# Causal attention on one core: the projections move into the attention slots, two head groups ahead, and each score tile gets a PSUM bank of its own

## The chip, the cores and the metric

The program runs on one core of a Trainium2 chip. The metric is the device time of one execution in microseconds; lower is better. Engines are named as in the profile: PE is TensorE, PEld its weight loads, DVE is VectorE, ACT is ScalarE, POOL is GpSimd, SP is the engine whose queue issues most DMAs.

## What is computed

Eight sequences of 1024 tokens, width 512, 16 heads of 32. An attention block, a layer norm, a mixture of 16 experts that each pick their tokens, a second layer norm. Only the attention block is touched:

```python
q = split_heads(x @ Wq.T + bq)
k = split_heads(x @ Wk.T + bk)
v = split_heads(x @ Wv.T + bv)
q_lr = jnp.einsum('bhtd,hdr->bhtr', q, Wq_lsr)
k_lr = jnp.einsum('bhtd,hdr->bhtr', k, Wk_lsr)
scores = jnp.einsum('bhir,bhjr->bhij', q_lr, k_lr) * scale
scores = jnp.where(causal_mask, jnp.float32(-jnp.inf), scores)
attn = jax.nn.softmax(scores, axis=-1)
y = jnp.einsum('bhij,bhjd->bhid', attn, v)
x = _layernorm(x + y @ Wo.T + bo)
```

## The kernel before

`build_attention` handles one sequence after the other (a "batch" in the code). The 16 heads go in four groups (`GROUPS`) of four heads (`HG`). One group is one **slot** of the program, and a batch is four slots and a **tail**.

For a group the kernel needs: the **projections** of its queries and keys ("proj", four of 12 matmuls each, every operand split into a high and a low float32r part); copies of them, the **strips**, which 24 DMAs on SP's queue bring from the tile `natural` into `q_operands` and `k_operands`, six per head, two buffers by the group's parity; the **row maxima** of the scores ("max", 48 matmuls whose tiles DVE reduces), joined and transposed ("maxT") and sent by two small DMAs into a row of `q_operands`, which is what `m_sent` counts; and the **core**: for 12 steps k the transposed scores of four heads ("scores"), their exponential on ACT, and two products, with the values ("values") and with ones for the denominators ("sums"). The denominators are inverted on DVE in four pieces and multiplied in on POOL.

The tail has for each of eight token tiles t the output product ("out"), layer norm 1 on DVE, the value projection of the next batch ("v"), the transposes of the normalised rows ("turn") and router logits ("logit").

PE's order is a list that `plan_batch` builds. All engines walk the same list, each taking its own part. In a slot g before the change come the four projections of group g+1, then the core of g, in which the 48 maxima of g+1 are spread evenly from step k=3 on, then maxT. Projections, maxima, maxT and the whole tail use two PSUM banks in turn (`shared`); a bank is free again when ACT or DVE has read it. The scores use four banks in two pairs: a pair holds two heads, and one ACT instruction of 1024 columns takes both. On the diagonal (8 of the 12 steps, so 32 score tiles in a slot) a matmul with `mask_k` adds the causal mask (line 630).

SP's queue holds DMAs in the order of its own code: strips, the weights of the next projection (`load_w`, 1 MB into the one buffer `wqk_group`), the next batch's x (`load_x`, into `natural`), and in the tail the residual rows (`x_residual`, two buffers) and the stores. POOL adds the bias to a residual tile before DVE may use it. SP, like every engine, does not go past an instruction that waits.

Of the kernel before, what the change touches and what calls it, by code (L numbers as in the profile page):

```python
# [15 lines left out]
P = 128  # L16
# [154 lines left out]
def plan_batch():  # L171

    order = []
    for g in range(GROUPS):
        order += plan_step(g, True)
    order += plan_tail()

    e = len(attend_steps())  # L180
    for g in range(GROUPS):
        n = order.index(("values", g, e - 1))
        order[n:n + 3] = [order[n + 2], order[n], order[n + 1]]
    return order


TURN_LAG = 2


def plan_tail():  # L190

    order = []
    for t in range(TT + TURN_LAG):
        if t < TT:
            order += [("out", t), ("v", t)]
        if t >= TURN_LAG:
            order.append(("turn", t - TURN_LAG))
            if (t - TURN_LAG) % QT == QT - 1:
                order.append(("logit", (t - TURN_LAG) // QT))
    return order  # L200


# [18 lines left out]
LEAD = 3  # L221
TAIL = 4


def attend_parts(g, k, e):


    parts = [("scores", g, k, 0), ("scores", g, k, 1)]
    for n in ([k - 1] if k > 0 else []) + ([k] if k == e - 1 else []):
        parts += [("values", g, n), ("sums", g, n)]  # L230
    return parts


def plan_step(g, attend):


    order = [("proj", g, i) for i in range(4)]
    e, m = len(attend_steps()) if attend else 0, len(max_steps())
    if not attend:
        return order + [("max", g, i) for i in range(m)] + [("maxT", g)]  # L240
    parts = [part for k in range(e) for part in attend_parts(g, k, e)]
    first, final = parts.index(("scores", g, LEAD, 0)), len(parts) - TAIL
    done = 0
    for n, part in enumerate(parts):
        order.append(part)
        if first <= n < final:
            share = m * (n + 1 - first) // (final - first)
            order += [("max", g, i) for i in range(done, share)]
            done = share
        if n == len(parts) - 3:  # L250
            order.append(("maxT", g))
    assert done == m
    return order


def build_attention(nc, w, x_dram, xT_dram, x1_dram, table, logits_dram, scratch, keep, NB):
    with ExitStack() as ctx:
# [80 lines left out]
        def turns(order, base):  # L338

            at, n = {}, base  # L340
            for item in order:
                if uses_bank(item):
                    at[item] = (n % 2, n // 2)
                    n += 1
# [1303 lines left out]
```

## Time and profile before

| | |
|---|---|
| median of 3 runs | 4426.57 us (4421.46 to 4427.38) |
| profiled execution | 4426.47 us, span 4424.7 us |
| PE busy | 3971.2 us, 90% of the span |
| PEld busy | 2624.6 us, 59% |
| DVE busy | 2281.6 us, 52% |
| ACT busy | 1423.9 us, 32% |
| POOL busy | 482.2 us, 11% |

The span is the time from the first to the last instruction of the profiled execution. Busy shares are averages over the whole program. The attention block takes roughly the first 2610 us of it; experts and the last layer norm fill the rest. Matmuls are pipelined, so "busy" counts overlapping pieces once and the distance from one matmul's start to the next says more than the length of either.

### The profile page before, as it was taken

Reading aid. Unit: us, or ns where it says so; the run is one execution under the profiler, and the core shown is the slowest. Engines: PE = TensorE matmul, PEld = TensorE weight load, DVE = VectorE, ACT = ScalarE, POOL = GpSimd, SP = SyncE. Lnnn points to the kernel's source line nnn. Section 1 sums busy time; section 2 is a strip of 40 time slices with the busy share of each in tenths; the row PEclk is TensorE's granted clock in tenths of the full one; section 3 lists DMA queues with packets and bytes.
Section 4 is the critical chain, followed back from the end, with each engine's and each line's share of the span. In section 5 each row is a group of like instructions: output and inputs, shape, how many; then the busy total and the mean of one; then the engine's idle time right before and its main releaser. Section 6 shows DMA issues by size and latency. Waiting matters only on the chain. (4 is left out here: it accounts for less than half of the span.)

```text
span 4424.7 us, 62103 instructions
## 1 busy us (share of the span) xinstructions
PE 3971.2 (90%) x22505; PEld 2624.6 (59%) x22505; DVE 2281.6 (52%) x3990; ACT 1423.9 (32%) x1986; POOL 482.2 (11%) x349
## 2 busy tenths in 40 slices
PE   5999999999999999999999971689999999999990
PEld 4545555555555455545555531578888888888880
DVE  2565455554554554554564546645444544454444
ACT  1233333332332332333333330133333333333324
POOL 2011011011011010011010010001111111111100
PEclk7899999999999999999999995589999999999995
DMA  4232323332331332133222310044433443344328
GB/s 139 61 84 87 76 70 96 79 79 76 77 101 56 76 101 82 51 100 92 66 82 84 73 55 8 7 138 129 126 117 117 126 129 117 117 125 130 117 67 313
DMA packets 187361, 423.09 MB, mean 96 GB/s; under 512 B 39776, under 2 KB 42848, under 8 KB 178400
## 3 DMA queue, kind: packets, MB, share of 16 engines
q1 hardware_dynamic: 167408, 367.98, 27.5%
q0 software_dynamic: 14336, 34.09, 4.1%
q10 hardware_dynamic: 5376, 17.83, 1.0%
q8 instruction: 149, 2.44, 0.2%
q14 instruction: 92, 0.75, 0.1%
HBM read 245.70 MB, written 72.38 MB: 72 GB/s over the span
## 5 line engine op out<-in xcount | busy, mean ns | idle before, releaser
L798 DVE TENSOR_REDUCE max_slots<-shared_banks 128x1 f32<-128x512 f32 (+3 forms) x1536 | 805.7, 550 | 632.6 <-PE shared_banks L581 535.6
L742 ACT ACTIVATE probs<-scores_t 128x1024 f32<-128x1024 f32 (+3 forms) x768 | 613.0, 811 | 907.4 <-PE scores_t L630 531.5
L1471 PE MATMUL m_ps_h<-m_tokens_t,m_w_parts 128*128 128x512 f32 x3072 | 739.8, 391 | 1.6 <-DVE m_tokens_t L1409 1.6
L1471 PE MATMUL m_ps_y<-m_w_parts,m_hidden_parts 128*128 128x512 f32 x3072 | 737.1, 390 | 0.5
L578 PE MATMUL shared_banks<-k_operands,q_operands 96*128 96x512 f32 (+3 forms) x1536 | 618.7, 431 | 63.9 <-DVE max_slots L798 52.7
L1471 PEld LDWEIGHTS m_ps_y<-m_w_parts,m_hidden_parts 128*128 128x128 f32 x3072 | 575.5, 188 | 125.3 <-issue 6.3
L1471 PEld LDWEIGHTS m_ps_h<-m_tokens_t,m_w_parts 128*128 128x128 f32 x3072 | 575.4, 188 | 120.1 <-issue 2.0
L578 PEld LDWEIGHTS shared_banks<-k_operands,q_operands 96*128 96x128 f32 x1536 | 295.9, 196 | 522.8 <-DVE max_slots L798 346.0
L627 PE MATMUL scores_t<-q_operands,k_operands 128*128 128x512 f32 (+3 forms) x1536 | 507.9, 403 | 21.3 <-ACT probs L742 15.4
L1378 ACT ACTIVATE m_hidden<-m_ps_h,m_b 128x512 f32<-128x512 f32 x256 | 176.7, 690 | 817.7 <-PE m_ps_h L1471 804.6
L1436 DVE CAST m_hidden_parts<-m_hidden 128x512 fp32r<-128x512 f32 x256 | 111.3, 435 | 584.1 <-ACT m_hidden L1378 584.1
L611 PE MATMUL shared_banks<-x_parts,wqk_group 128*128 128x512 f32 x1536 | 382.1, 406 | 22.1 <-issue 20.4
L611 PEld LDWEIGHTS shared_banks<-x_parts,wqk_group 128*128 128x128 f32 x1536 | 294.5, 195 | 95.6 <-issue 28.3
L627 PEld LDWEIGHTS scores_t<-q_operands,k_operands 128*128 128x128 f32 x1536 | 290.0, 198 | 88.6 <-issue 47.9
L647 PE MATMUL y_bank<-probs,v_rows 128*32 128x512 f32 (+3 forms) x3072 | 336.1, 510 | 0.0
L647 PE MATMUL den_bank<-probs,ones_f 128*32 128x512 f32 (+3 forms) x3072 | 328.9, 500 | 0.0
L493 POOL TENSOR_TENSOR y_cols<-y_cols,denominators 128x512 f32<-128x512 f32 x64 | 82.0, 1281 | 1660.5 <-DVE denominators L826 1660.5
L611 PE MATMUL shared_banks<-wo_cols,y_cols 128*128 128x512 f32 x512 | 236.9, 606 | 15.7 <-DVE ln_stats L837 8.1
L581 PE MATMUL shared_banks<-mask_q_rows,ident_bf 128*128 128x128 bf16 x1024 | 242.3, 237 | 0.0
L1336 POOL DMA_INDIRECT scratch_x<-m_out,m_idx x64 | 114.0, 1781 | 1142.9 <-DVE m_out L1455 1128.3
L826 DVE RECIPROCAL denominators<-denominators 128x128 f32<-128x128 f32 x256 | 235.9, 936 | 2.2
L630 PE MATMUL scores_t<-mask_k_rows,ident_bf 128*128 128x128 bf16 x1024 | 230.6, 231 | 0.0
(206 smaller groups left out, 3318.2 us busy)
## 6 DMA issues: line engine op xcount, KB each, us to landing
m_w_raw<-in_w1T SPq DMA_DIRECT2D x64, 1024.0 KB, 5.1
m_w_raw<-in_w2T SPq DMA_DIRECT2D x64, 1024.0 KB, 7.3
q_operands<-natural SPq DMA_DIRECT2D x384, 128.0 KB, 2.4
k_operands<-natural SPq DMA_DIRECT2D x384, 128.0 KB, 2.5
wqk_group<-scratch_wqk SPq DMA_DIRECT2D x32, 1024.0 KB, 5.2
natural<-in_xT SPq DMA_DIRECT2D x8, 2048.0 KB, 7.6
x_residual<-in_x SPq DMA_DIRECT2D x64, 256.0 KB, 2.7
scratch_x<-probs SPq DMA_DIRECT2D x64, 256.0 KB, 2.0
```

The lines of the kernel that those rows point to most:

```text
L578: mm = pe.matmul(out[:, 0:n], q_ops[0:MAX_STRIP, buf, h, it * P:(it + 1) * P], k_ops[0:MAX_STRIP, buf, h, k0:k0 + n], start=True, stop=not ...
L581: mm = pe.matmul(out[:, n - P:n], identb[:], mask_q[:], start=False, stop=True)
L611: mm = pe.matmul(out, a, c, start=(n == 0), stop=(n == len(pairs) - 1))
L627: mm = pe.matmul(out[:, c0:HALF], k_ops[:, buf, h, j * P:(j + 1) * P], q_ops[:, buf, h, hh * HALF + c0:(hh + 1) * HALF], start=True, stop= ...
L630: mm = pe.matmul(out[:, c0:c0 + P], identb[:], mask_k[:], start=False, stop=True)
L647: mm = pe.matmul(bank[h * DH:(h + 1) * DH, c0:HALF], rows(h, j), probs[:, slot_of(k, h // 2), h % 2, c0:HALF], start=(j == 0), stop=(j == ...
L742: act.activation(probs[:, slot_of(k, pair), :, c0:HALF], st[:, pair, :, c0:HALF], ACT.Exp, scale=SCALE).then_inc(exp_done, 1)
L798: dve.tensor_reduce(mx[:, h, slot:slot + 1], src[:, 0:n], AX.X, ALU.max).then_inc(bank_free[bank], 1)
L826: dve.reciprocal(den[:, cols], den[:, cols]).then_inc(rden_ready, 1)
L1336: pool.indirect_dma_start(out=x1_dram[:, :], out_offset=bass.IndirectOffsetOnAxis(ap=idx[:, r, j:j + 1], axis=0), in_=out[:, j, :], in_off ...
L1378: act.activation(h[:, f % 2, :], ps_h[:, f % 2, 0:CAP], ACT.Gelu, bias=b1[:, r, f:f + 1]).then_inc(gelu_done, 1)
L1471: mm = pe.matmul(bank, a, b, start=(first and n == 0), stop=(final and n == len(pairs) - 1))
```

## The change

The projections of a group are made two slots ahead and inside the core, two of them after part 46 and two after part 57 of the 60 parts of a slot. The strips then go into the buffer that the running core still reads, so SP waits for the slot's last score tile (`st_full`) before it issues them. The 48 maxima are placed by a table, the first of them after part 5, that is after the second head of step k=1. Scores have four single banks: one matmul, one ACT instruction and one wait for each head. The causal mask is no longer a matmul; POOL zeroes the upper triangle of the probabilities after the exponential (`mask_probs`, one instruction for two heads), and "values" of a diagonal step waits for it. "values" and "sums" of a step stand side by side. The pieces of the inversion have fixed places. The next batch's x is split on POOL in eight pieces during slot 2. On SP's queue one set of strips, for group 1 of the next batch, now stands in the tail. The lead-in makes two groups and mixes values, projections and maxima.

```diff
-LEAD = 3
-TAIL = 4
-        if n == len(parts) - 3:
-            order.append(("maxT", g))
+AHEAD = 2
+MAX_AFTER = (0, 0, 0, 0, 0, 2, 1, 1, 0, 1, 1, 0, 0, 1, 0, 1, 0, 0, 5, 2,
+             3, 1, 2, 0, 1, 1, 0, 1, 1, 1, 1, 0, 2, 2, 0, 0, 0, 1, 3, 2,
+             2, 0, 2, 1, 0, 1, 1, 0, 1, 1, 0, 1, 1, 0, 0, 0, 0, 0, 0, 0)
+PROJ_AFTER = (46, 46, 57, 57)
+JOIN_AFTER = 55
...
+    for k in range(e):
+        parts += [("scores", k, h) for h in range(HG)]
+        if k > 0:
+            parts.append(("weigh", k - 1))
...
+            order += [("values", g, part[1]), ("sums", g, part[1])]
...
-        st = ps("scores_t", [P, 2, 2, HALF])
+        st = ps("scores_t", [P, SCORE_BANKS, HALF])
...
-            def strips(b, g, lead=False):
-                await_parts(sp, sp_passed, b, (g - 1) % GROUPS, lead)
+            def strips(b, slot, lead=False):
+                await_parts(sp, sp_passed, b, slot, lead)
+                g = (slot + AHEAD) % GROUPS
+                if not lead:
+                    plain(sp, st_full, (b * GROUPS + slot + 1) * NE * HG, sp_passed)
...
                 if more:
-                    load_x(b + 1, n0 + GROUPS)
-                    load_w(0)
-                    strips(b, 0)
+                    load_x(b + 1, b * GROUPS + GROUPS)
+                    strips(b, GROUPS - 2)
                     load_w(1)
-                for t in range(TT + TURN_LAG):
+                load_residual(b, 0)
+                if more:
+                    strips(b, GROUPS - 1)
+                    load_w(2)
+                for t in range(1, TT + TURN_LAG):
...
+            def mask_probs(b, g, k, pair):
+                c0 = steps[k][2]
+                s = (b * GROUPS + g) * NE + k
+                block = probs[:, slot_of(k, pair), :, c0:c0 + P]
+                plain(pool, exp_done, HG * s + 2 * pair + 2 + SCORE_BANKS, pool_passed)
+                pool.affine_select(out=block, in_=block, compare_op=ALU.is_ge, fill=0.0, base=0,
+                                   pattern=[[0, 2], [1, P]], channel_multiplier=-1).then_inc(masked, 1)
...
-                for q in range(2):
-                    h = 2 * pair + q
-                    out = st[:, pair, q, :]
-                    diag = j * P >= hh * HALF
-                    mm = pe.matmul(out[:, c0:HALF], k_ops[:, buf, h, j * P:(j + 1) * P],
-                                   q_ops[:, buf, h, hh * HALF + c0:(hh + 1) * HALF], start=True, stop=not diag)
-                    if diag:
-                        mm = pe.matmul(out[:, c0:c0 + P], identb[:], mask_k[:], start=False, stop=True)
-                mm.then_inc(st_full, 1)
+                pe.wait_ge(exp_done, s + 1)
+                pe.matmul(st[:, (HG * k + h) % SCORE_BANKS, c0:HALF], k_ops[:, buf, h, j * P:(j + 1) * P],
+                          q_ops[:, buf, h, hh * HALF + c0:(hh + 1) * HALF], start=True, stop=True).then_inc(st_full, 1)
...
+                if diagonal[k]:
+                    pe.wait_ge(masked, (b * GROUPS + g) * N_DIAG + masked_through(k))
```

What this does to the order is seen at three places. The first is PE's order from the end of one slot into the next, before the change; the line numbers are those of the kernel before (L611 projections, L647 values and sums, L627 scores, L630 their mask).

```order
L647 MATMUL y_bank<-probs,v_rows 32x128 x4
L647 MATMUL den_bank<-probs,ones_f 32x128 x4
L611 MATMUL shared_banks<-x_parts,wqk_group 128x512 x12
L527 REGISTER_ALU
L611 MATMUL shared_banks<-x_parts,wqk_group 128x512 x24
L620 REGISTER_ALU
L622 ISA
L627 MATMUL scores_t<-q_operands,k_operands 128x512
L630 MATMUL scores_t<-mask_k_rows,ident_bf 128x128
```

The same place after the change (L670 projections, L701 values and sums, L682 scores):

```order
L670 MATMUL shared_banks<-x_parts,wqk_group 128x512 x12
L693 REGISTER_ALU
L701 MATMUL y_bank<-probs,v_rows 32x256 x4
L701 MATMUL den_bank<-probs,ones_f 32x256 x4
L693 REGISTER_ALU
L694 ISA
L701 MATMUL y_bank<-probs,v_rows 32x128 x4
L701 MATMUL den_bank<-probs,ones_f 32x128 x4
L679 REGISTER_ALU
L681 ISA
L682 MATMUL scores_t<-q_operands,k_operands 128x512
```

The last projection of a slot, whose result the strips carry, stood right ahead of the next slot's scores; now the products of steps 10 and 11 stand between.

The second place is the start of a slot on PE after the change, from the fourth head of step 0 on. L637 is a maximum, L640 its mask.

```order
L682 MATMUL scores_t<-q_operands,k_operands 128x512
L681 ISA
L682 MATMUL scores_t<-q_operands,k_operands 128x384
L681 REGISTER_ALU
L682 MATMUL scores_t<-q_operands,k_operands 128x384
L634 REGISTER_ALU
L637 MATMUL shared_banks<-k_operands,q_operands 128x128
L640 MATMUL shared_banks<-mask_q_rows,ident_bf 128x128
L584 REGISTER_ALU
L637 MATMUL shared_banks<-k_operands,q_operands 128x256
```

The first maximum, which waits for head 0 of the strips, now comes after six score tiles; before, the scores of steps 0 to 2 and half of step 3 and the products of steps 0 to 2 stood ahead of it.

The third place is SP's queue around the start of the tail. Before, the last strips and the weights were followed by the two first residual loads:

```order
L387 DMA wqk_group<-scratch_wqk 128x2048
L414 REGISTER_ALU
L415 ISA
L415 DMA x_residual<-in_x 128x512
L415 ISA
L415 DMA x_residual<-in_x 128x512
```

After the change the first residual load stands ahead of the 24 strips of slot 3 (rows like these two, twelve times), and the second one behind them and behind the weights:

```order
L441 DMA x_residual<-in_x 128x512
L49 REGISTER_ALU x2
L49 ISA
L435 DMA q_operands<-natural 32x1024
L436 DMA k_operands<-natural 32x1024
```

```order
L435 DMA q_operands<-natural 32x1024
L436 DMA k_operands<-natural 32x1024
L422 DMA wqk_group<-scratch_wqk 128x2048
L441 ISA
L441 DMA x_residual<-in_x 128x512
```

The residual load for the second token tile was free to go long before the tail began; it has moved behind 25 DMAs that start only when slot 3 is over.

## Rows read from the trace of the kernel before

**Rows 1.** Busy time by stage: one slot, its start, the lead-in, a batch's first projections.

```profile
core 0: us, PE busy (x) PEld busy (x) DVE busy (x) ACT busy (x) POOL busy (x), PEclk, DMA share, GB/s
792.55:855.20 62.65, 60.07 (x402) 32.57 (x401) 36.64 (x65) 23.30 (x31) 1.38 (x2) 1.00 0.28 69
792.55:801.19 8.64, 7.92 (x62) 3.84 (x60) 0.75 (x1) 5.33 (x7) 0.00 (x0) 1.00 0.55 121
91.64:149.02 57.38, 44.68 (x129) 27.52 (x130) 29.10 (x55) 4.30 (x6) 0.00 (x0) 0.61 0.30 74
778.39:792.55 14.16, 13.93 (x48) 10.94 (x49) 2.25 (x3) 3.35 (x4) 0.00 (x0) 0.80 0.01 2
```

**Rows 2.** Timeline of PE, end of a slot: start, length, line, operation.

```profile
846.29 0.42 PE L647 MATMUL y_bank<-probs,v_rows 128*32 128x128 f32 x8
846.87 8.50 PE L611 MATMUL shared_banks<-x_parts,wqk_group 128*128 128x512 f32 x36
```

**Rows 3.** Timeline of PE inside a slot: scores with and without mask, values and sums.

```profile
793.18 0.48 PE L627 MATMUL scores_t<-q_operands,k_operands 128*128 128x512 f32 x1
793.54 0.48 PE L627 MATMUL scores_t<-q_operands,k_operands 128*128 128x512 f32 x1
...
796.38 1.07 PE L647 MATMUL y_bank<-probs,v_rows 128*32 128x512 f32 x8
797.26 1.04 PE L647 MATMUL den_bank<-probs,ones_f 128*32 128x512 f32 x8
...
805.69 0.63 PE L627 MATMUL scores_t<-q_operands,k_operands 128*128 128x512 f32 x2
806.16 0.40 PE L578 MATMUL shared_banks<-k_operands,q_operands 96*128 96x512 f32 x1
...
816.97 1.06 PE L647 MATMUL y_bank<-probs,v_rows 128*32 128x512 f32 x8
817.97 0.56 PE L578 MATMUL shared_banks<-k_operands,q_operands 96*128 96x512 f32 x2
```

**Rows 4.** Timeline of SP's queue, the strips of two slots.

```profile
798.25 0.58 SPq L397 DMA_DIRECT2D k_operands<-natural  x1
...
856.97 0.52 SPq L396 DMA_DIRECT2D q_operands<-natural  x1
...
860.07 0.59 SPq L397 DMA_DIRECT2D k_operands<-natural  x1
...
872.56 0.59 SPq L387 DMA_DIRECT2D wqk_group<-scratch_wqk  x1
```

**Rows 5.** DMA issues: count, KB each, median us from issue to landing.

```profile
k_operands<-natural SPq DMA_DIRECT2D x384, 128.0 KB, 2.5
wqk_group<-scratch_wqk SPq DMA_DIRECT2D x32, 1024.0 KB, 5.2
...
x_residual<-in_x SPq DMA_DIRECT2D x64, 256.0 KB, 2.7
```

**Rows 6.** Timeline of PE in a tail: first and third output product, next batch.

```profile
714.17 3.70 PE L611 MATMUL shared_banks<-wo_cols,y_cols 128*128 128x512 f32 x8
...
727.49 3.60 PE L611 MATMUL shared_banks<-wo_cols,y_cols 128*128 128x512 f32 x8
...
778.39 8.32 PE L611 MATMUL shared_banks<-x_parts,wqk_group 128*128 128x512 f32 x24 [3.02 <-issue]
```

**Rows 7.** Groups by shape: count, busy us, mean ns, idle before.

```profile
L798 DVE TENSOR_REDUCE max_slots<-shared_banks 128x1 f32<-128x512 f32 x768 | 516.6, 688 | 153.4 <-PE shared_banks L578 90.7 <-PE shared_banks L581 57.4
L742 ACT ACTIVATE probs<-scores_t 128x512 f32<-128x512 f32 x128 | 73.0, 597 | 157.7 <-PE scores_t L630 157.7
L997 POOL TENSOR_SCALAR_AFFINE_SELECT s_same_expert<-s_same_expert 128x128 f32<-128x128 f32 x1 | 0.4, 399 | 0.1
```

**Rows 8.** Timelines of DVE and POOL in a tail: statistics, bias onto the residual.

```profile
718.82 0.69 DVE L837 BATCH_NORM_STATS2 ln_stats<-probs 128x6 f32<-128x512 f32 x1
...
721.58 1.66 POOL L506 TENSOR_TENSOR x_residual<-x_residual,bo_folded 128x512 f32<-128x512 f32 x1 [32.00 <-DMA x_residual<-in_x]
```

More of the change, by code:

```diff
@@ L220 @@
 DEN_PIECES = 4
-LEAD = 3
-TAIL = 4
[L225 to L242, printed above, removed]
-    done = 0
[L244 to L249, printed above, removed]
-        if n == len(parts) - 3:
-            order.append(("maxT", g))
-    assert done == m
-    return order
+TURN_LAG = 2
@@ new lines, in plan_slot @@
+def plan_slot(g):
+    order, done = [], 0
+    for n, part in enumerate(core_parts()):
+        if part[0] == "scores":
+            order.append(("scores", g) + part[1:])
+        else:
+            order += [("values", g, part[1]), ("sums", g, part[1])]
+        order += [("proj", g, i) for i, at in enumerate(PROJ_AFTER) if at == n]
+        order += [("invert", g, 0, i) for i, at in enumerate(INVERT_AFTER[0]) if at == n]
+        if g > 0:
+            order += [("invert", g - 1, 1, i) for i, at in enumerate(INVERT_AFTER[1]) if at == n]
+        order += [("max", g, i) for i in range(done, done + MAX_AFTER[n])]
+        done += MAX_AFTER[n]
+        if n == JOIN_AFTER:
+            order.append(("maxT", g))
+    assert done == len(max_steps())
+    return order
@@ new lines, in plan_lead @@
+def plan_lead():
+    g, m = GROUPS - AHEAD, len(max_steps())
+    order = [("proj", g, i) for i in range(4)] + [("v", 0), ("v", 1)]
+    fill = [("v", t) for t in range(2, TT)]
+    for i in range(4):
+        fill.insert(2 * i + 1, ("proj", g + 1, i))
+    done = 0
+    for n, item in enumerate(fill):
+        order.append(item)
+        share = m * (n + 1) // len(fill)
+        order += [("max", g + 1, i) for i in range(done, share)]
+        done = share
+    return order + [("maxT", g + 1)]
@@ L256, in build_attention, with plan_batch @@
+def plan_batch():
+    order = []
+    for g in range(GROUPS):
+        order += plan_slot(g)
+    return order + plan_tail()
 def build_attention(nc, w, x_dram, xT_dram, x1_dram, table, logits_dram, scratch, keep, NB):
@@ L321, in build_attention, with masked_through @@
         batch = plan_batch()
-        lead_in = [("v", t) for t in range(TT)] + plan_step(GROUPS - 1, False)
-        uses_bank = lambda item: item[0] not in ("scores", "values", "sums")
-        N_LEAD = sum(map(uses_bank, lead_in))
-        N_BATCH = sum(map(uses_bank, batch))
-        assert N_BATCH % 2 == 0
+        lead_in = plan_lead()
+        uses_bank = lambda item: item[0] not in ("scores", "values", "sums", "invert")
+        diagonal = [j * P >= hh * HALF for hh, j, _ in steps]
+        N_DIAG = 2 * sum(diagonal)
+        def masked_through(k):
+            return 2 * sum(diagonal[:k + 1])
         def slot_of(k, pair):
@@ L801, in run @@
                         n = 0 if lead else b * GROUPS + item[1] + 1
-                        for k in range(2):
-                            dve.wait_ge(bank_free[k], off + (turn if k == bank else turn_of_other(at[item])))
+                        for k, before in enumerate(seen_by(b, item, lead)):
+                            dve.wait_ge(bank_free[k], off[k] + before)
                         dve.tensor_copy(mrow[:, :, 0:4], mx[:, :, 0:4]).then_inc(mx_joined, 1)
```

225 lines of the change are left out of this document (117 added, 108 removed).

## The prediction, made before the changed kernel ran

> **What bounds the kernel now.** I read the stages first, then PE's timeline inside one slot. In a slot of 62.65 us PE is busy 60.07, DVE 36.64, ACT 23.30 [rows 1]. PE is the bound, and only what PE does or waits for counts. All 32 slots of the attention block look alike, and a tail follows each four. The one stretch with visible slack on PE is a slot's start: its first 8.64 us hold 7.92 of work [rows 1]. There PE has scores and products of steps 0 to 2 to do while the strips of the next group travel; the first maximum comes at 801.19, just when head 0 is there. So the question about the change is what it takes off PE, and where PE now stands before something that is not there yet. I count from T0, the end of a slot's last projection; before the change that is the first score tile of the next slot, 792.55 or 855.20.
>
> **Taken off PE.** (a) The masks of the scores. Two score tiles with masks start 0.36 us apart (793.18, 793.54), two without take 0.47 together (805.69 to 806.16), so 0.235 each [rows 3]: a mask costs 0.125 at 512 columns. With fewer columns the bare tile cannot get much shorter than its weight load lets it, so I take 0.07 as the mean of the 32 masks, 2.2 us a slot; the bounds are 1.2 (a third of the full price) and 4.0 (the full price for all). (b) "values" and "sums" side by side: 0.88 us from one to the other (796.38, 797.26), 1.00 when a maximum follows (816.97, 817.97) [rows 3]. Eight steps of a slot had a maximum between. I price a separation at three times this 0.12: leaving the products, the maximum's own weights that could not load ahead, entering the products again. That is 2.9 us a slot, an estimate with bounds 1.0 and 3.5. Together 5.1 us a slot; over 31 slots' worth (the last one had no maxima) -158 us, bounds -70 and -230.
>
> The Trainium skill, "TensorE: Matmul & The Clock Gate", section "Step-by-step: what each phase is for", says that PE pulls weight loads ahead of running matmuls. By that rule a mask would cost its 128 columns alone, an estimate of 0.053 us each or 1.7 us a slot, and the sum would be 16 us higher. The rows show 0.125 at 512 columns, so here the load of a mask's weights is not hidden.
>
> **Added: PE waits for the strips.** A set of strips starts 1.77 us after T0 (855.20 to 856.97), when ACT and DVE have read the last projection. The sixth DMA, the last of head 0, starts at 860.07 in one slot and 798.25 in the other [rows 4] and lands 2.5 later [rows 5]: T0+7.4 and T0+8.2, mean 7.8. The new condition, all scores of the slot done, is met before T0. Between T0 and the first maximum PE now has the products of steps 10 and 11 (step 11: 0.58, from 846.29 to 846.87 [rows 2]; step 10, twice the columns, 1.0), four score tiles of 0.235 and two shorter ones of 0.2: 3.0 us. So it stands for 4.8 us where it stood for 0.7 (8.64 less 7.92): +4.1 in each of slots 1 to 3, 23 times in the program: +94 us. Slot 0 is free of it: its strips travel in the tail before it. Bounds: 3.6 and 5.0 each, from the two landings. Behind the waiting maximum stand all later scores; ACT has six tiles, 3.6 us at 0.597 [rows 7], and then waits too. Heads 1 to 3 land 4 us apart and are hidden.
>
> **Added: the second residual tile.** In the seven batches that are followed by another, SP's queue has 24 strips and the weights ahead of the residual of token tile 1. From 856.97 to 872.56 the strips take 15.6 us [rows 4]; so the weights go at T0+17.4 and the residual at T0+18.0. It lands at T0+20.7 (2.7 alone) or, behind the weights' 5.2, at about T0+23.3 [rows 5]. POOL adds the bias in 1.66, DVE adds and measures in twice 0.69 [rows 8], and only then the bank of the second output product is free: T0+23.7 to T0+26.3. PE wants that bank for the third output product. It starts the tail at T0+1.6, and from the first to the third took 13.3, of which 0.6 were step 11's products (714.17, 727.49 [rows 6]): T0+14.3. PE stands for 9.4 to 12.0 us; I take 11.2, since the DMA engines are full then: +78 us. Before, this load had landed long ahead. POOL's bias addition and DVE's layer norm are queued in order behind it, the next residuals are not late any more.
>
> **Smaller terms.** Slot 0 now begins with scores whose banks ACT frees at 0.597 a tile, after PE did four in 0.94: about 1.5 us, +12 in eight batches (0 to 25). The maxima keep DVE's 0.688 each at 512 columns [rows 7], but the table puts 13 between parts 18 and 22 and ten between 33 and 42. For 13 of them DVE needs up to 8.9 us, about 6.9 with the narrow ones (an estimate), PE at most 13 times 0.36, 4.7, and two banks cover about 1 of the difference; an even spread had less of that: +0.7 a slot, +22 (0 to 45). ACT pays its fixed part twice as often (48 of 0.597 against 24 of about 1.02 in a slot) and stays below half busy: nothing. POOL's masks: 128 columns took 0.399 [rows 7], so 0.4 to 0.8 for 256; they come after the exponential and before "values", which has four further score tiles and the previous products ahead of it, some 3 us: nothing, and if that cover were gone 0.8 per step, 32 x 8 x 0.8 = 205 us at worst. The lead-in from 91.64 to 149.02 has PE busy 44.68 of 57.38 [rows 1] and gets work mixed in, but its own projections also wait for strips: -8 (0 to -20).
>
> **The clock.** After the tail PE waited 3.02 us (778.39 [rows 6]), and in the next 14.16 us the granted clock was 0.80 on average [rows 1], that is 2.4 GHz with a stretch at 1.2. The same 48 matmuls at full clock take 48/36 of 8.33 (846.87 to 855.20), 11.1 [rows 2]: one such fall costs 3.1 where PE is dense. The new waits are longer than this one. There are 30 of them, and I take 1.0 each, since what follows most of them are small tiles in which PE was not dense anyway: +30 us, bounds 0 and 93. The Trainium skill, "TensorE: Matmul & The Clock Gate", section "What's actually happening", has the clock follow how busy PE was; the trace agrees, with 0.80 behind a wait.
>
> **Sum.** -158 +94 +78 +12 +22 -8 +30 = +70. The profiled execution took 4426.47 us (4424.7 of span and 1.8 around it), the median is 4426.57, so nothing is to be converted: 4426.5 + 70 = 4497 us.
>
> **Rivals.** *Forecast*: both waits as priced, slower by 70; chance 0.5, and its own range is 4460 to 4535. *The clock decides* (slower by more): every one of the 30 waits costs the full 3.1, 93 instead of 30: 4560. The rule of the Trainium skill's clock page, named above, leads here, since it follows from a pause alone. For it speaks the 0.80 behind a mere 3.02 us; against it that small tiles were bound by weights and banks. Chance 0.2. *POOL is late*: x is split on POOL in slot 2 between the masks of step 3 and of step 8, and the masks queue behind inversions that DVE does late; if half the diagonal steps wait 0.6, that is +75, 4570. For it speaks that POOL's order is fixed and each of its waits holds all that follows; against it its 1.38 us of work in a slot [rows 1]. Chance 0.1. *The residual is not late* (the other side): its wait and the clock after it vanish, -78 and -7, and the work taken off is 6 us a slot, -28 more: 4384. The case turns at waits and clock together: they are 202 us in the sum, and under 132 the change is no loss, which needs one of the two waits nearly gone. For it speaks that DMAs overlap; against it that SP issues in order and 25 issues take 16 us by themselves. Chance 0.15. *Nothing to be seen*: savings at 5.1 and waits at their lower bounds meet, chance 0.05.
>
> **How the numbers follow.** This kernel's runs tell apart about 0.2%, 9 us. The time is that of the likeliest case, 4497. From 4405 (savings at 6 us a slot, waits at their lower bounds, no clock loss: -186 +83 +66 +12 +10 -8 +0, about -20) to 4570 (clock and POOL) the range leaves some 2 in 10 outside. Slower: 0.5 + 0.2 + 0.1 = 0.8. Faster 0.15, same 0.05.
>
> **What would show it.** PE's first maximum of slots 1 to 3 waits 3.6 to 5 us for the strips; the third output product waits 9 to 12 for DVE in seven tails; slots 1 to 3 last within 2 us of 62.65 while PE's busy time in them falls by about 4; scores start 0.235 apart on the diagonal at 512 columns; more and longer stretches at half clock. Wrong would be the forecast if slots shrink below 60 us, which means that savings are larger or that strips come sooner, if the tail is not longer than before, or if "values" waits for POOL.

## The result, and the profile after

The changed kernel took 4498.91 us (median; 4497.29 to 4503.71), the kernel before 4425.82 (4421.46 to 4427.38) beside it: a ratio of 1.0169, 95% interval 1.0151 to 1.0186, 73 us slower. The forecast was 4497. The profiled execution spans 4496.4 us.

The page of the kernel after, two of its costliest groups (line, engine, operation, count, busy time, mean ns, idle time just before it and what ended most of it).

```profile
L637 PE MATMUL shared_banks<-k_operands,q_operands 96*128 96x512 f32 (+3 forms) x1536 | 603.8, 415 | 136.7 <-DMA k_operands<-natural 90.5
...
L670 PE MATMUL shared_banks<-wo_cols,y_cols 128*128 128x512 f32 x512 | 255.0, 645 | 107.8 <-DVE ln_stats L880 98.8
```

Two causes stand behind nearly all new idle time of PE, and they are the two that the forecast named: the maxima (L637) wait 90.5 us for strips, the output products (L670) 98.8 us for DVE's statistics. Before, the two lines had 7.3 and 8.1 us of such waits. The waits of PE by line and releaser (total us, times, longest) say how often:

```profile
PE shared_banks L670 <- DVE ln_stats L880: 98.8, 11, 13.9
PE shared_banks L637 <- DMA k_operands<-natural: 90.5, 24, 4.3
PE scores_t L682 <- issue: 25.3, 6, 4.6
PE shared_banks L637 <- DVE max_slots L845: 20.5, 71, 0.5
```

Windows of the kernel after (columns as in [rows 1]): a slot 0 with the loop's boundary ahead of it, a slot 1, slot 1 from T0 to its first maximum, what PE does of that, the 4 us behind the wait, the wait in the tail, the products behind it, the lead-in, and the whole attention block.

```profile
811.20:873.58 62.38, 56.11 (x337) 31.89 (x337) 31.63 (x59) 24.76 (x54) 7.74 (x17) 0.92 0.01 3
873.58:935.25 61.67, 56.58 (x370) 31.92 (x369) 36.56 (x65) 24.67 (x55) 8.94 (x18) 0.97 0.28 70
873.58:881.02 7.44, 3.52 (x39) 1.94 (x38) 3.21 (x4) 4.01 (x8) 1.22 (x3) 1.00 0.57 124
873.58:877.22 3.64, 3.52 (x39) 1.94 (x38) 2.69 (x4) 2.75 (x6) 0.33 (x1) 1.00 0.18 38
881.02:885.04 4.02, 4.01 (x18) 2.16 (x22) 2.42 (x5) 0.98 (x2) 0.41 (x1) 0.58 0.92 207
1075.33:1088.82 13.49, 0.00 (x2) 0.00 (x1) 1.39 (x2) 0.00 (x0) 2.48 (x2) 0.64 0.83 230
1088.82:1093.90 5.08, 5.08 (x8) 2.25 (x9) 1.72 (x5) 0.96 (x3) 1.57 (x1) 0.61 0.43 155
90.00:161.29 71.29, 53.49 (x169) 35.98 (x169) 26.84 (x51) 5.90 (x10) 0.00 (x0) 0.76 0.24 60
160.00:2680.00 2520.00, 2234.53 (x13458) 1262.69 (x13459) 1325.78 (x2434) 899.34 (x2012) 465.36 (x693) 0.94 0.28 76
```

The slot shrank from 62.65 us [rows 1] to 61.67 and PE's work in it from 60.07 to 56.58: 3.5 us were taken off, and 2.5 came back as waiting.

But [rows 1] is a slot 0 and this is a slot 1, and single slots differ by more than 1 us. From a slot's first score tile to that of the next, on the mean of all batches, slot 0 went from 63.33 to 59.95 us, slot 1 from 62.81 to 62.28, slot 2 from 62.57 to 60.99, and slot 3 with its tail from 129.04 to 142.37 in the seven batches that have a next one. In sum slots 0 win 27 us, slots 1 and 2 together 17, and slots 3 with their tails, where PE stands still for 13.49 us, lose 93. The lead-in loses 12 more and the last slot 3 with its tail 2: 64 us up to the start of the selection, which is at 2663.56 before (the attention block with its last tail ends there, not at roughly 2610) and at 2727.13 after; the other 8 us of the profiled runs lie behind it.

Over the attention block the granted clock is 0.94; before, the same window reads:

```profile
160.00:2680.00 2520.00, 2359.82 (x14594) 1298.65 (x14593) 1353.44 (x2483) 857.00 (x1256) 271.17 (x196) 0.98 0.29 79
```

Taking 1.00 for 2.4 GHz and 0.50 for 1.2, that is 2 x 0.02 x 2520 = 101 us at the lower level before and 302 us after, each within 25 us, since the clock is given to two digits.

How the wait for strips arises, in PE's timeline (start, length, line, operation, idle before):

```profile
867.98 5.67 PE L670 MATMUL shared_banks<-x_parts,wqk_group 128*128 128x512 f32 x24
...
875.02 2.20 PE L682 MATMUL scores_t<-q_operands,k_operands 128*128 128x512 f32 x6
881.02 0.38 PE L637 MATMUL shared_banks<-k_operands,q_operands 96*128 96x128 f32 x1 [3.80 <-DMA k_operands<-natural]
```

and in SP's queue, the first and the sixth strip, the last of head 0:

```profile
875.44 0.54 SPq L435 DMA_DIRECT2D q_operands<-natural  x1
...
878.56 0.59 SPq L436 DMA_DIRECT2D k_operands<-natural  x1
```

T0 is 873.58, where the 24 projection products end and the products of step 10 start. The strips start 1.9 us later, the sixth 5.0 us later, and it lands after some 2.5 more: 881.0, when PE goes on. The tail of the same kernel, SP, POOL, DVE and PE one after the other:

```profile
1079.00 0.58 SPq L422 DMA_DIRECT2D wqk_group<-scratch_wqk  x1
1079.81 0.96 SPq L441 DMA_DIRECT2D x_residual<-in_x  x2
```

```profile
1086.05 2.48 POOL L567 TENSOR_TENSOR x_residual<-x_residual,bo_folded 128x512 f32<-128x512 f32 x2 [10.83 <-DMA x_residual<-in_x]
```

```profile
1087.35 0.69 DVE L878 TENSOR_TENSOR probs<-shared_banks,x_residual 128x512 f32<-128x512 f32 x1 [13.50 <-POOL x_residual L567]
```

```profile
1068.93 3.60 PE L670 MATMUL shared_banks<-wo_cols,y_cols 128*128 128x512 f32 x8
...
1088.82 5.65 PE L670 MATMUL shared_banks<-wo_cols,y_cols 128*128 128x512 f32 x8 [13.49 <-DVE ln_stats L880]
```

Read it upward: PE waits for DVE, DVE 13.50 us for POOL, POOL for a transfer that SP issued only at 1079.81, behind 24 strips and the weights. The eight products behind the wait take 5.65 us where the eight before it took 3.60, at a granted clock of 0.61.

### The profile page after: what moved, and what is told of

Its sections match the earlier page's. It is cut to its first block and busy times, and to the rows that moved or that the text cites. A ratio compares the mean times of both kernels' runs of the same rounds, so it can differ in the third digit from the quotient of the medians.

```text
span 4496.4 us, 63955 instructions
## 1 busy us (share of the span) xinstructions
PE 3868.6 (86%) x21481; PEld 2605.4 (58%) x21481; DVE 2279.3 (51%) x3990; ACT 1468.2 (33%) x2754; POOL 681.1 (15%) x859
## 5 line engine op out<-in xcount | busy, mean ns | idle before, releaser
L796 ACT ACTIVATE probs<-scores_t 128x512 f32<-128x512 f32 (+3 forms) x1536 | 667.2, 495 | 870.2 <-PE scores_t L682 818.0
L637 PE MATMUL shared_banks<-k_operands,q_operands 96*128 96x512 f32 (+3 forms) x1536 | 603.8, 415 | 136.7 <-DMA k_operands<-natural 90.5
L682 PE MATMUL scores_t<-q_operands,k_operands 128*128 128x512 f32 (+3 forms) x1536 | 522.3, 400 | 41.2 <-issue 25.3
L637 PEld LDWEIGHTS shared_banks<-k_operands,q_operands 96*128 96x128 f32 x1536 | 302.2, 199 | 408.4 <-issue 149.1
L541 POOL TENSOR_SCALAR_AFFINE_SELECT probs<-probs 128x256 f32<-128x256 f32 x512 | 206.7, 406 | 1607.1 <-ACT probs L796 1601.9
L670 PE MATMUL shared_banks<-x_parts,wqk_group 128*128 128x512 f32 x1536 | 371.8, 398 | 23.0 <-DVE x_parts L901 18.9
L682 PEld LDWEIGHTS scores_t<-q_operands,k_operands 128*128 128x128 f32 x1536 | 292.0, 203 | 153.7 <-issue 95.7
L701 PE MATMUL y_bank<-probs,v_rows 128*32 128x512 f32 (+3 forms) x3072 | 347.9, 526 | 2.1 <-POOL probs L541 1.8
L670 PE MATMUL shared_banks<-wo_cols,y_cols 128*128 128x512 f32 x512 | 255.0, 645 | 107.8 <-DVE ln_stats L880 98.8
L670 PEld LDWEIGHTS shared_banks<-x_parts,wqk_group 128*128 128x128 f32 x1536 | 288.1, 191 | 93.4 <-issue 33.8
L701 PE MATMUL den_bank<-probs,ones_f 128*32 128x512 f32 (+3 forms) x3072 | 325.4, 496 | 0.0
L640 PE MATMUL shared_banks<-mask_q_rows,ident_bf 128*128 128x128 bf16 x1024 | 248.2, 242 | 0.0
L670 PEld LDWEIGHTS shared_banks<-wo_cols,y_cols 128*128 128x128 f32 x512 | 100.3, 205 | 227.2 <-issue 113.4
```

The source lines that it names most:

```text
L541: pool.affine_select(out=block, in_=block, compare_op=ALU.is_ge, fill=0.0, base=0, pattern=[[0, 2], [1, P]], channel_multiplier=-1).then_i ...
L637: mm = pe.matmul(out[:, 0:n], q_ops[0:MAX_STRIP, buf, h, it * P:(it + 1) * P], k_ops[0:MAX_STRIP, buf, h, k0:k0 + n], start=True, stop=not ...
L640: mm = pe.matmul(out[:, n - P:n], identb[:], mask_q[:], start=False, stop=True)
L670: mm = pe.matmul(out, a, c, start=(n == 0), stop=(n == len(pairs) - 1))
L682: pe.matmul(st[:, (HG * k + h) % SCORE_BANKS, c0:HALF], k_ops[:, buf, h, j * P:(j + 1) * P], q_ops[:, buf, h, hh * HALF + c0:(hh + 1) * HA ...
L701: mm = pe.matmul(bank[h * DH:(h + 1) * DH, c0:HALF], rows(h, j), probs[:, slot_of(k, h // 2), h % 2, c0:HALF], start=(j == 0), stop=(j == ...
```

## The experiments

Each states its change against the kernel after unless it says before. A chunk is one of the 12 steps k of a slot. All were timed beside the kernel before, whose medians were 4425.71, 4424.75 and 4428.0 in the three sets. To make a difference to the kernel after, its 4498.91 us are used.

**The residual's request ahead of the strips.** The strips of the last slot go out head by head behind the requests of residual tiles 2 to 5, not as a block of 24 ahead of tile 1.

```
-                if more:
-                    strips(b, GROUPS - 1)
-                    load_w(2)
                 for t in range(1, TT + TURN_LAG):
...
+                    if more and 0 <= t - TURN_LAG < HG:
+                        strips(b, GROUPS - 1, heads=(t - TURN_LAG,))
```

> The changed kernel, with SP's order in the tail alone undone: the 24 strips of slot 3 go one head (six DMAs) at a time behind the stores of token tiles 0 to 3, the weights behind the last, so the residual tiles are never behind them. Forecast's account: PE's wait for the bank of the second output product (12.5 to 13.9 us in the changed kernel's trace, seven times) is gone, and with it the stretch at half clock behind it: 4499 less 7 x 13 and less 7 to 15 for the clock, about 4397 (4385 to 4415). Rival, the wait comes from something else in the tail (the inversion pieces or POOL's normalisation ahead of layer norm): no more than 20 us gained, above 4479. Rival, strips spread thin arrive late and the first maxima of slot 0 wait instead: gain under 60.

Measured: 4412.1 us, ratio 0.9971 (0.9961 to 0.9982). 87 us less than after, and by itself enough to turn the loss into a small gain. Forecast's account holds, and its 4397 was 15 too low. In its waits the strips keep their 90.5, and the output products' wait for the statistics falls by 72.8 to

```profile
PE shared_banks L672 <- DVE ln_stats L882: 26.0, 11, 4.6
```

where the kernel before had 8.1. The other 14 of the 87 us are no waiting; that they are the clock is the likely reading, which this run alone doesn't show.

**The first maxima one chunk later.** Of the table only the first row changes.

```
-MAX_AFTER = (0, 0, 0, 0, 0, 2, 1, 1, 0, 1, 1, 0, 0, 1, 0, 1, 0, 0, 5, 2,
+MAX_AFTER = (0, 0, 0, 0, 0, 0, 0, 0, 2, 1, 1, 1, 0, 2, 0, 1, 0, 0, 5, 2,
```

> The changed kernel with the first eight entries of the table of maxima moved: the first maximum comes after part 8 (the products of step 0) and not after part 5; the other 40 stay. Forecast's account: PE waits 3.8 us (over the matmul's own end) for head 0 of the strips 23 times; with the products of step 0 (1.9 us) and two more score tiles ahead of it the wait shrinks to under 1, but ACT and POOL set the pace of steps 0 and 1 and take back part: 1.5 to 2.5 us gained each, and up to 1 of clock: 4499 less 35 to 80, about 4445. Rival, the strips are not what slot starts wait for but ACT's pace: no change, 4490 to 4505. Rival, maxima pushed together make DVE late in the cluster behind: slower than 4499.

Measured: 4451.9 us, ratio 1.0058 (1.0042 to 1.0075), 47 us less. The waits show why it is no more:

```profile
PE shared_banks L637 <- DVE max_slots L845: 42.4, 122, 0.5
...
PE shared_banks L637 <- DMA k_operands<-natural: 20.5, 24, 3.1
```

70 us of waiting for strips went, and 22 us of waiting for DVE came, since the same maxima now stand closer together: 48 net. Slots 0 had no wait for strips to lose: there the move only costs, 61.3 us on the mean for 59.9.

**Work in the waits.** 16 matmuls whose output nobody reads stand before the first maximum of slots 1 to 3, 50 before the third output product of the seven tails. They fill most of the two waits and change nothing in when transfers are requested.

```
+                    if item == ("out", 2) and not (isinstance(b, int) and b == NB - 1):
+                        busy(st[:, 0, :], 50)
...
+                        if item[2] == 0 and not lead and g > 0:
+                            busy(out, 16)
```

> The changed kernel with matmuls on constant weights, whose results are overwritten, put into PE's two waits: 16 (3.6 us at full clock) ahead of the wait for head 0 of the strips in slots 1 to 3, 50 (11.4 us) ahead of the third output product in seven tails. They fit into the waits and keep PE busy, so what the time loses is what the clock costs behind the waits. The forecast's term: -30 us, 4469. Rival that the clock decides (3.1 us for each of 30 waits): -93, 4406. Rival that the clock costs nothing behind a wait: 4499 or a few us more. The granted clock of the stretches behind the waits should be 1.00.

Measured: 4446.47 us, ratio 1.005 (1.0033 to 1.0067), 52 us less, by doing more work. The same window as above:

```profile
160.00:2680.00 2520.00, 2371.34 (x14364) 1389.25 (x14364) 1341.21 (x2472) 907.29 (x2033) 474.52 (x708) 0.98 0.29 78
```

The granted clock is back at 0.98, that of before. So the clock's share of the loss was 52 us (a lower bound, if the added matmuls at places outlast the wait): neither the 30 of the forecast nor the 93 of the rival, and nearer to the forecast. Behind the filled waits the granted clock is 1.00 (868.35 to 872.37 and 1070.61 to 1075.69 of this run), as expected, and the eight products there take 3.70 us for 5.65. It also says what a microsecond at the lower level costs here: 52 / (302 - 101), about a quarter of one (0.2 to 0.35 with the rounding of the clock).

**Before, without the masks of the scores.** This one starts from the kernel before and leaves out the causal mask of the score tiles.

```
-                                   q_ops[...], start=True, stop=not diag)
-                    if diag:
-                        mm = pe.matmul(out[:, c0:c0 + P], identb[:], mask_k[:], start=False, stop=True)
+                                   q_ops[...], start=True, stop=True)
```

> The kernel before, without the 32 matmuls of a slot that add the causal mask to the score tiles (the upper triangle of the diagonal blocks stays in; nothing takes the mask's place). It prices the first part of what the change takes off PE. Forecast: 2.2 us a slot, 32 slots, -70 us: 4356 (bounds 4387 and 4298). By the rule that weight loads are pulled ahead of running matmuls a mask is 128 columns, 0.053 us: -54, 4372. Rival, other engines pace the steps and PE's saving is not seen: under -25, above 4400.

Measured: 4380.57 us, ratio 0.9897 (0.988 to 0.9913): 45 us less, 1.4 a slot, not 2.2. Its waits take the rest back:

```profile
PE shared_banks L578 <- DVE max_slots L796: 64.3, 164, 1.0
PE scores_t L627 <- ACT probs L740: 35.9, 63, 2.2
...
PE shared_banks L578 <- DMA k_operands<-natural: 10.7, 6, 7.3
```

In the kernel before these are:

```profile
PE shared_banks L578 <- DVE max_slots L798: 52.7, 133, 1.0
PE scores_t L627 <- ACT probs L742: 15.4, 32, 1.7
...
PE shared_banks L578 <- DMA k_operands<-natural: 7.3, 1, 7.3
```

That is 35.5 us of new waits in a run that ought to win 70. Work removed just ahead of a wait only lengthens the wait: 14 of a slot's 32 masks stand ahead of its first maximum, where PE has little to do while ACT works off their tiles. 1.4 is thus a lower bound of what the masks cost PE; with the new waits it would be 80 us, 2.5 a slot.

**The masks put back on TensorE.** The same term from the other side: the kernel after, POOL's masks kept, and TensorE's added again.

```
-                          q_ops[...], start=True, stop=True).then_inc(st_full, 1)
+                               q_ops[...], start=True, stop=not diagonal[k])
+                if diagonal[k]:
+                    mm = pe.matmul(out[:, c0:c0 + P], identb[:], mask_k[:], start=False, stop=True)
+                mm.then_inc(st_full, 1)
```

> The kernel after with TensorE's masks of the scores put back beside POOL's (term a undone). Term a as predicted, 2.2 us a slot: 68 us more than 4499, 4567. Taken out of the kernel before, the same masks gave 45 us, since those of the slot's first chunks lie in front of a wait for the strips; here 6 of 32 do in three slots of four: 45 to 60 us more, 4544 to 4559. Rival (weight load pulled ahead, 1.7 us a slot, less those hidden): 40 us more, 4539.

Measured: 4582.18 us (4575.83 to 4593.88), ratio 1.035 (1.032 to 1.0379): 83 us more, 2.7 a slot, 0.084 us for each of 31 x 32 masks. The forecast's 0.07 was right within a fifth. By the Trainium skill, "TensorE: Matmul & The Clock Gate", section "Step-by-step: what each phase is for", weight loads are pulled ahead of running matmuls; the 1.7 us a slot that the prediction worked out from it are further away than 2.2, so here that rule did not hide the masks' loads.

**Before, values and sums adjacent.** From the kernel before, one condition more: no maximum behind a "values".

```
-        if first <= n < final:
+        if first <= n < final and part[0] != "values":
```

> The kernel before with one edit: no operation of the maxima is placed between a chunk's value products and its sums, so that the two stand back to back as in the kernel after. My theory (term b of the prediction): 2.9 us per slot x 31 slots = 90 us less, so about 4336 us against 4426. Bounds from the prediction's 1.0 to 3.5 us per slot: 31 to 108 us less. Since the term for the masks came out at 1.4 instead of 2.2 us per slot when it was tried alone, I lean to less than 90. Rival: the separation costs nothing by itself and the long values products of before were the clock or the neighbouring maxima: then 4426 within 10.

Measured: 4492.5 us, ratio 1.0151 (1.0125 to 1.0177): 68 us *slower*. Both theories missed. The edit did a second thing that I had not counted: the maxima that had stood behind "values" were bunched with those behind "sums". DVE takes 0.688 us for a full one [rows 7], two banks hold them, and its inversions of 0.94 us stand in the same queue. In the waits,

```profile
PE shared_banks L578 <- DVE max_slots L798: 124.2, 168, 2.2
```

against 52.7 in the row of before above: 71.5 us of new waiting. This run doesn't say what adjacency is worth; it says what an uneven spread of the maxima costs.

**One maximum back between values and sums.** A cleaner form, from the kernel after: in the seven chunks of a slot that have a maximum behind the sums, one of them goes in front of the sums.

```
-            order += [("values", g, part[1]), ("sums", g, part[1])]
+            between = MAX_AFTER[n] > 0
+            order += [("values", g, part[1])] + [("max", g, done)] * between + [("sums", g, part[1])]
```

> The kernel after with one maximum put back between the value products and the sums of seven of the twelve chunks in each slot; nothing else moves, and no maxima are bunched. Term b of the prediction prices a separation at 0.36 us: 7 x 31 x 0.36 = 78 us more than 4499. The rows of the kernel before read again give 0.23 (the value products take 0.99 instead of 0.88 us, and the sums start 0.16 instead of 0.04 us after a mask): 50 us more, 4549. Rival: adjacency is worth nothing by itself, as the run that made the two adjacent in the kernel before seemed to say: 4499 within 9.

Measured: 4567.07 us (4565.98 to 4570.4), ratio 1.0316 (1.0294 to 1.0338): 68 us more, 0.31 for each of 7 x 31 separations. The forecast had 0.36. PE's timeline of this run shows a chunk with the maximum between:

```profile
939.80 0.50 PE L639 MATMUL shared_banks<-k_operands,q_operands 96*128 96x512 f32 x1
940.23 1.07 PE L703 MATMUL den_bank<-probs,ones_f 128*32 128x512 f32 x8
```

Its value products had started at 938.80, so they hold 1.00 us to themselves, as in [rows 3], where an adjacent pair has 0.88; and the maximum holds 0.43, where two neighbouring ones in the kernel before took 0.73 together:

```profile
826.47 0.80 PE L578 MATMUL shared_banks<-k_operands,q_operands 96*128 96x512 f32 x2
827.20 1.06 PE L647 MATMUL y_bank<-probs,v_rows 128*32 128x512 f32 x8
```

These two steps make 0.12 + 0.06 = 0.18 of the 0.31, 39 us of the 68. Another 17 are waits for DVE, which the moved maxima brought along: 33.2 us where the kernel after has 20.5, and 12.8 for DVE's copies of the projections (`natural`) where it has 8.4.

```profile
PE shared_banks L639 <- DVE max_slots L847: 33.2, 132, 0.5
```

So this run is not as clean as it was meant to be, and the 0.31 is the price of a separation with the waits it causes, some 0.23 without them. Where the last 12 us go isn't shown.

**Without POOL's masks.** It leaves out the causal mask and the wait for it.

```
-                    if item[0] == "scores" and diagonal[item[2]] and item[3] % 2 == 1:
-                        mask_probs(b, item[1], item[2], item[3] // 2)
...
-                if diagonal[k]:
-                    pe.wait_ge(masked, (b * GROUPS + g) * N_DIAG + masked_through(k))
```

> The kernel after without POOL's masks on the probabilities and without the wait for them; it leaves out the causal mask. Theory of the prediction: POOL's masks are hidden, so 4494 to 4502 us, no change from 4499. Rival (POOL late): each slot's first values wait for the masks, up to 2.4 us per slot, 75 us less, 4425.

Measured: 4490.24 us (4485.5 to 4492.6), 9 us less, at the edge of what the measurement tells. POOL being late is out. And the 9 are not the masks' either, as far as the traces tell: the profiled run of this kernel reaches the selection at 2726.71 us, that of the kernel after at 2727.13, and the rest of its gain (its span is 4490.7 for 4496.4) lies behind the attention block, where nothing was edited (the experts get other data, since the mask is left out). In the kernel after one mask is 0.41 us and PE's products wait 1.8 us for them in all:

```profile
L541 POOL TENSOR_SCALAR_AFFINE_SELECT probs<-probs 128x256 f32<-128x256 f32 x512 | 206.7, 406 | 1607.1 <-ACT probs L796 1601.9
...
L701 PE MATMUL y_bank<-probs,v_rows 128*32 128x512 f32 (+3 forms) x3072 | 347.9, 526 | 2.1 <-POOL probs L541 1.8
```

**The lead-in in another order.** First projection, all the v products, then the other projection, then the maxima in one piece.

```
+     order += [("v", t) for t in range(2, TT)] + [("proj", g + 1, i) for i in range(4)]
+     return order + [("max", g + 1, i) for i in range(m)] + [("maxT", g + 1)]
```

> The kernel after with the lead-in in another order: the strips' maxima do not stand behind the projection whose eviction is the last that they wait for. Theory: the lead-in's three uncovered waits (4.3, 5.0, 3.3 us) are cut to a half or less, about 12 us less than 4499, so 4487 (4480 to 4495). Rival: the waits only move to another place of the lead-in: 4499 within 4.

Measured: 4478.63 us (4476.16 to 4481.2), 20 us less. The batch's first scores, at 161.29 in the kernel after, come at 143.56:

```profile
143.56 2.07 PE L674 MATMUL scores_t<-q_operands,k_operands 128*128 128x512 f32 x4 [3.61 <-DMA q_operands<-minus_max]
```

That is 17.7 of the 20 us. The theory was right in direction and too small: of the waits ahead of the lead-in's maxima for DVE's copies of the projection (4.31, 1.31, 1.43 and 1.38 us in the kernel after) one of 1.43 is left, the one of 3.34 for the strips is gone, and the one for the shift by the maxima, 5.04, is 3.61. These make 11.8 of the 17.7.

**Three edits together**: the residual's request, the first maxima, the lead-in.

> The kernel after with three edits together: the second residual tile's request first (alone 87 us less), the first maxima of each slot one chunk later (alone 47 us less), and the lead-in's other order (expected 12 us less). If the waits are separate, the gains add up: 4499 - 87 - 47 - 12 = 4353 us (4340 to 4370). Rival: part of each gain was the clock, which is granted once for both, so that together they give less: 4375 to 4390.

Measured: 4365.2 us (4363.0 to 4368.68), ratio 0.9859 (0.9834 to 0.9884). It beats the kernel before by 60 us, 1.4%. The gains are 134 us where apart they were 87, 47 and 20, 154 together: between the two theories, with the first nearer. The two waits add up as if alone: 18.5 us are left for strips and 25.5 for statistics, where the single runs left 20.5 and 26.0. That the missing 20 are the clock, won once and not twice, I did not test.

**The last projection earlier.** From the run with three edits:

```
-PROJ_AFTER = (46, 46, 57, 57)
+PROJ_AFTER = (46, 46, 53, 53)
```

> The run with all three edits (4365 us) with the last two quarters of the projection four places earlier, before the slot's last scores. Theory: the strips then start when the last scores are done and not 1.8 us after the last projection, so the wait for strips that is left (18.5 us in all) nearly goes, 4365 - 15 - some clock = 4345. Rival: the strips wait for the last scores anyway, which now stand where the last projection stood, so that they start only 1 us earlier, and DVE, which copies the projections, has its maxima late at the place to which they moved: 4365 within 10.

Measured: 4490.04 us (4488.14 to 4495.61), 125 us worse than the run it starts from. Both theories missed. What the first one promised came: PE's waits for strips (18.5 us) are gone from the list. But the waits name two new ones, 31 times each:

```profile
PE y_bank L695 <- POOL probs L535: 62.6, 31, 3.2
PE shared_banks L637 <- DVE row_max L847: 53.7, 31, 1.8
```

116 us in all. In PE's timeline:

```profile
985.49 5.73 PE L664 MATMUL shared_banks<-x_parts,wqk_group 128*128 128x512 f32 x24
...
993.22 0.28 PE L637 MATMUL shared_banks<-ident_f,row_max 128*32 128x128 f32 x1 [1.83 <-DVE row_max L847]
...
996.67 0.65 PE L695 MATMUL y_bank<-probs,v_rows 128*32 128x128 f32 x8 [1.83 <-POOL probs L535]
```

and in DVE's:

```profile
991.98 0.75 DVE L832 SCALAR_TENSOR_TENSOR natural<-shared_banks,bk_cols,natural 128x512 fp32r<-128x512 f32 x1 [1.97 <-ACT natural L738]
992.84 0.17 DVE L846 COPY row_max<-max_slots 128x16 f32<-128x16 f32 x1
```

The joining of the maxima stands on DVE behind the projection's copies, which wait for ACT; and the projection, 5.7 us of PE's time, was what lay between the last scores and the last values while ACT and POOL did exponential and mask. The prediction had priced POOL's masks at nothing *because of a cover*; here the cover is gone and the price comes due, 2.0 us a slot.

## Why the prediction was right, point by point

The total was right within 2 us; its terms were less so, and their errors cancelled.

- **Masks (a), -68.** 83 when undone in the kernel after. Right, a fifth too small.
- **Adjacency (b), -90 for eight separations.** Seven put back cost 68, so eight are about 78, some 15 of them the waits for DVE that the next term counts too. Right in kind, too large.
- **The maxima on DVE, +22.** Wrong sign: PE's waits for them fell from 52.7 us to 20.5, -32. The step that failed is "an even spread had less of that". The spread of before was even in parts of the order, but DVE's inversions fell between its maxima. In DVE's timeline of before an inversion of 0.95 us stands in front of the maximum that PE needs:

```profile
808.49 0.95 DVE L826 RECIPROCAL denominators<-denominators 128x128 f32<-128x128 f32 x1
809.36 0.36 DVE L798 TENSOR_REDUCE max_slots<-shared_banks 128x1 f32<-128x256 f32 x1
```

and PE stands 0.97 us at 809.77. 28 such waits of over 0.9 us make 27 of the 52.7. The prediction had called a slot's start, with 0.72 us, the one stretch with visible slack on PE; this row of the same slot held more. The new order gives the inversions places of their own, which fits the fall; no run moved the inversions alone, so it is argued and not shown. The step is this: I had priced the moved maxima and not the moved inversions.

- **Strips, +94.** The mechanism is as forecast, 23 waits that end at T0+7.4, and one in the lead-in. PE stands 3.8 and not 4.8 us, since the work ahead of the first maximum took 3.6 and not 3.0: the six score tiles took 2.20 and not 1.34, with ACT at work on one after the other (its six exponentials take 2.83 us from 875.65 on, 0.48 from one to the next and not the 0.597 that one takes). Less the 0.7 of before it is 3.1 x 23 = 71.
- **Residual, +78.** 12.44 to 13.92 us in the seven tails, 91 in all: just outside my bounds of 9.4 to 12.0. PE wanted the bank at T0+14.4 (forecast 14.3; this T0 is 1060.89), SP's request went at T0+18.9 (18.0), and it landed 6.2 us after that. This landing is what was mis-sized: I had taken 2.7 to 5.3, and with strips and weights under way (the 16 engines' busy share is 0.83) it took longer. The run with the request first gives 87 for what it took of wait and clock together.
- **Clock, +30.** 52 by the run with work in the waits. It was mis-sized at both places. In the tail the products behind the wait are dense, 5.65 against 3.60 us. But small tiles pay too: with the waits filled, slots 1 and 2, which have one wait for strips each, are 1.6 us shorter on the mean, and slot 3 with its tail 4.3, where I had taken 1.0 for every wait. The Trainium skill, "TensorE: Matmul & The Clock Gate", section "What's actually happening", has the clock follow how busy PE was. The trace agrees: with PE busy and the transfers where they were, the granted clock is 0.98 for 0.94.
- **Lead-in, -8.** Wrong sign: the first scores came at 161.29 and not 149.02. Mixed in, the maxima wait for copies of projections that in turn wait for strips (ACT's first copy, at 89.90, had waited 12.90 us for them); the other order takes 20 back.
- **Slot 0, +12.** A wait for ACT of 0.92 us in eight batches, 7. **POOL, 0.** As forecast: PE's products wait 1.8 us for it in all, and without its masks the selection starts 0.4 us sooner.

With these sizes the sum is -83 -78 -32 +71 +91 +52 +12 +7 = +40 of 73. Five more are the last batch's tail, which is 73.4 us from its first output product (2653.70) to the selection (2727.13) where it was 68.5 (2595.11 to 2663.56); five the issue waits of PE at the loop's boundary (25.3 for 20.4 in all); eight lie behind the attention block (below). That is 58. Some 15 are counted twice as savings, in adjacency and in DVE's waits; counted once, the sum is 73. I would not lean on so close a fit: each size comes from an edit of its own, and their errors are several us each.

So the total owes its closeness to luck: DVE and the strips came out 77 us below their terms, masks and adjacency together 3, slot 0 5; residual, clock and lead-in 55 above, 18 are things that had no term, and 15 the overlap. What held is the structure: the savings inside the slots are real and larger than each wait alone, and two requests that come late on SP's queue eat them. The two runs that move a request or its user show it: 87 and 47 us, with the savings left in place.

## What to carry to other kernels

When work is reordered on the bound engine, list what each of its first uses after the move waits for, and follow that back through the queue that issues it; here one load behind 24 others on a queue cost more than all masks saved. Take such a wait away by issuing in the order of need before touching the compute. And test a term of the sum by an edit that moves one thing only: a queue in order, like DVE's, turns "one less here" into "two in a row there".

## What the runs showed of the hardware that I had not expected

Matmuls that nobody reads, put where PE would stand still, made the kernel 52 us faster, at an unchanged order of transfers: a wait of 13.5 us costs its length and then 2.0 us more on the next eight products.

Code that the change doesn't touch got slower. In the selection behind the attention block, one round of the counting loop takes 6.51 us after (2784.97 to 2791.48 on PE, in the kernel after) and 6.28 before (2744.98 to 2751.26). In both PE waits for DVE most of that time, 5.93 and 5.69 us. DVE's instructions last as long as before, but two of them start later behind their predecessor. After:

```profile
2786.83 0.22 DVE L1180 COPY_PREDICATED_SCALAR s_threshold<-s_keep,s_candidates 128x1 int32 x1 [0.25 <-DVE s_threshold L1180]
2787.54 0.16 DVE L1167 TENSOR_TENSOR s_candidates<-s_threshold,s_bits 128x3 int32<-128x3 int32 x1 [0.49 <-DVE s_threshold L1180]
```

Before:

```profile
2746.75 0.22 DVE L1137 COPY_PREDICATED_SCALAR s_threshold<-s_keep,s_candidates 128x1 int32 x1 [0.15 <-DVE s_threshold L1137]
2747.32 0.16 DVE L1124 TENSOR_TENSOR s_candidates<-s_threshold,s_bits 128x3 int32<-128x3 int32 x1 [0.35 <-DVE s_threshold L1137]
```

That is 0.10 and 0.14, the whole 0.24 of a round. It goes with the program and not with chance: the median round is 6.27 or 6.28 us in the traces of the kernel before and its two variants, and 6.51 in all ten of the kernel after and its variants, at a granted clock of 0.50 during the rounds in all of them. The 16 rounds make about 3.5 us. From the start of the selection to the end of the span it is 8 us longer (4496.4 - 2727.13 against 4424.7 - 2663.56). Why the gaps on DVE grew, and where the rest of the 8 comes from, isn't known; no run here was made for it.
